# A top-k threshold search laid out by tokens, with seven candidates a round counted by TensorE, and one shared-expert group moved behind it

## The reference

```python
scores = jax.nn.sigmoid(h @ gate_w.T)                    # 2048 tokens x 16 experts
cap = math.ceil(T / E * TOP_K)                           # 256
topk_score, topk_ids = jax.lax.top_k(scores.T, cap)      # every expert takes 256 tokens
xin = h[topk_ids]
up = jnp.einsum('ecd,efd->ecf', xin, up_w) + up_b[:, None, :]
g = jnp.einsum('ecd,efd->ecf', xin, gw) + gb[:, None, :]
eo = jax.nn.silu(g) * up                                 # 512 hidden features
eo = jnp.einsum('ecf,edf->ecd', eo, down_w) + down_b[:, None, :]
flat = (eo * topk_score[..., None]).reshape(-1, Dm)
out = jnp.zeros_like(h).at[topk_ids.reshape(-1)].add(flat)
shared = jax.nn.silu(x @ sh_gate_w.T) * (x @ sh_up_w.T)  # 256 hidden features
out = out + shared @ sh_down_w.T
```

## Time and profile before

| what | value |
|---|---|
| timed runs, median of 3 | 206.12 us |
| profiled execution, span (first to last instruction) | 204.6 us |
| PE / PEld busy | 181.2 / 156.4 us |
| VectorE busy | 125.5 us |
| ScalarE busy | 90.3 us |
| GpSimd busy | 127.5 us |
| TensorE clock, mean over the span | 0.966 of full speed |

### The profile page before, as it was taken

One profiled execution on the slowest core, in us unless ns is written; L12 is line 12 of the kernel. 1 busy time (PEld: TensorE's weight loads), 2 busy tenths in 40 slices (PEclk: granted clock), 3 DMA queues, 4 the chain that ended last, 5 costly groups with the idle time before them and its releaser, 6 DMA issues.

```text
span 204.6 us, 3620 instructions
## 1 busy us (share of the span) xinstructions
PE 181.2 (89%) x1196; PEld 156.4 (76%) x1196; DVE 125.5 (61%) x430; ACT 90.3 (44%) x239; POOL 127.5 (62%) x195
## 2 busy tenths in 40 slices
PE   6979898999979999998999999999999999957800
PEld 6947688999936677857899999999999889945700
DVE  4888999999878787785667644454445344422300
ACT  0687512448697768110344344444444345422210
POOL 7494005556117475927777888878878777866660
PEclk9999999999999999999999999999999999995875
DMA  5599999800030271104313323333233333332221
GB/s 149 182 411 419 420 419 419 363 12 3 0 117 0 99 225 51 49 23 138 91 44 42 43 42 45 54 40 42 43 47 53 40 40 29 40 40 21 20 24 13
DMA packets 11649, 22.26 MB, mean 109 GB/s; under 512 B 1504, under 2 KB 8800, under 8 KB 11504
## 3 DMA queue, kind: packets, MB, share of 16 engines
q1 hardware_dynamic: 5968, 17.52, 22.7%
q0 software_dynamic: 5664, 4.53, 16.1%
HBM read 17.72 MB, written 4.33 MB: 108 GB/s over the span
## 4 chain that ended last, share of the span: by engine, by line
PE 41%; DMA 15%; POOL 14%; issue 11%; DVE 10%; ACT 4%; POOLq 1%; SPq 1%; DVEq 0%; ACTq 0%
DMA out_dram<-area,rows 13%; POOL out_dram L542 9%; PE bank L1155 7%; PE bank L1434 4%; PE bank L1110 4%; PE bank L1435 4%; POOL hT L531 4%; PE bank L1296 4%; PE bank L1415 3%; PE bank L1308 3%; DMA x_tok<-in_x_dram 2%; PE bank L1258 2%; DVE junk L950 1%; DVE area L807 1%; DVE hT L817 1%
## 5 line engine op out<-in xcount | busy, mean ns | idle before, releaser
L542 POOL DMA_INDIRECT out_dram<-area,rows x32 | 50.7, 1584 | 16.8 <-DMA out_dram<-area,rows 8.7
L1086 DVE SCALAR_TENSOR_TENSOR area<-bank,consts,sgate 128x256 f32<-128x256 f32 x64 | 30.9, 483 | 42.4 <-ACT sgate L734 42.1
L734 ACT ACTIVATE sgate<-bank,consts 128x256 f32<-128x256 f32 x64 | 30.3, 473 | 53.3 <-PE bank L1435 53.1
L1434 PE MATMUL bank<-area,wT 128*128 128x256 f32 x128 | 40.3, 397 | 4.8 <-issue 4.1
L1415 PEld LDWEIGHTS bank<-wT,area 128*128 128x128 f32 x256 | 38.1, 191 | 4.1 <-DVE area L1086 1.0
L531 POOL DMA_INDIRECT hT<-h_rows,rows x32 | 31.9, 995 | 12.7 <-issue 9.1
L1435 PE MATMUL bank<-area,wT 128*128 128x256 f32 x128 | 39.3, 390 | 0.0
L1415 PE MATMUL bank<-wT,area 128*128 128x128 f32 x256 | 38.6, 275 | 0.6 <-DVE area L1086 0.6
L1435 PEld LDWEIGHTS bank<-area,wT 128*128 128x128 f32 x128 | 25.2, 197 | 3.7
L1434 PEld LDWEIGHTS bank<-area,wT 128*128 128x128 f32 x128 | 20.5, 198 | 6.2 <-issue 5.7
L518 POOL TENSOR_TENSOR sh_hid<-sh_up,sgate 128x64 f32<-128x64 f32 x48 | 13.7, 322 | 14.6 <-ACT sh_up L686 12.1
(11 more groups left out here) (195 smaller groups left out, 259.1 us busy)
## 6 DMA issues: line engine op xcount, KB each, us to landing
wT<-in_weights_dram SPq DMA_DIRECT2D x16, 768.0 KB, 16.2
h_rows<-hrow SPq DMA_DIRECT2D x2, 576.0 KB, 3.7
x_tok<-in_x_dram SPq DMA_DIRECT2D x4, 256.0 KB, 3.9
x_tok<-in_down_b_dram SPq DMA_DIRECT2D x1, 1024.0 KB, 6.2
out_dram<-x SPq DMA_DIRECT2D x4, 256.0 KB, 2.1
hT<-h_rows,rows POOLq DMA_INDIRECT x32, 2.6
out_dram<-area,rows POOLq DMA_INDIRECT x32
sh_wT<-in_shared_dram SPq DMA_DIRECT2D x1, 384.0 KB, 2.9
```

Of the source, the lines that this page charges most:

```text
L542: pool.indirect_dma_start(out=out_rows, in_=eo[:, e % 2, c, :], in_offset=None, out_offset=bass.IndirectOffsetOnAxis(ap=rows[:, c, e:e + 1 ...
L734: act.activation(sgate_e[:, q % SGB, :], up_bank(q)[:, CAP:2 * CAP], ACT.Silu, bias=biasT[:, 1, j, e:e + 1]).then_inc(s_sil, 1)
L1086: dve.scalar_tensor_tensor(hidden[:, e % 2, j, :], up_bank(q)[:, 0:CAP], biasT[:, 0, j, e:e + 1], sgate_e[:, q % SGB, :], ALU.add, ALU.mul ...
L1434: pe.matmul(up_bank(q)[:, 0:CAP], wT[:, e, 0, j, :], xselT[:, e % 2, :], start=True, stop=True)
```

## The change

The scores stay as the router makes them: a partition holds 16 tokens with 16 experts each, 256 values, so nothing is turned. VectorE copies the high halves into `key_hi`. A round tries seven candidates (three bits) or three (two bits): one comparison of every key with every candidate, spread over the middle dimension, fills `over` with ones and zeros in 16 bits, 1792 or 768 per partition, in three pieces or two. TensorE multiplies a matrix of ones with `over`, 16 matmuls that add up in one PSUM row block, so that every partition gets all totals. VectorE compares them with 256, adds up the steps and makes the next candidates. There are eleven rounds: 8, 8, 8, 8, 4 for the high half and 8, 8, 8, 8, 4, 4 for the low one; between them `key_lo` is made by subtraction, joining and clamping. ScalarE counts no more. The masks come out by tokens and need no turning; column counts for the ranks go through TensorE and a copy of one column.

In the shared expert, groups 0 and 1 are projected in rounds 0 to 7, with outputs in rounds 6 to 10. Group 2 moves behind the search, with its product on VectorE (L1039 of the new file) instead of GpSimd, ahead of group 3. The warm-up matmuls in the rounds, ahead of the first table and behind the last spread are gone.

```diff
-        ROUNDS = [b for b in range(BITS - LOW - 2, -1, -2)] + [b for b in range(LOW - 2, -1, -2)]
+        ROUNDS = ((8, 2048), (8, 256), (8, 32), (8, 4), (4, 1), (8, 8192), (8, 1024), (8, 128), (8, 16), (4, 4), (4, 1))
+        ROUNDS_HIGH = 5
+        PIECES = {8: (0, 6, 12, 16), 4: (0, 10, 16)}
...
-            for n in range(LAST):
+            for n in range(LAST - 1):
                 for t in range(SHT):
                     pool.wait_ge(s_shsil, SHT * n + t + 1)
                     pool.wait_ge(s_shupe, SHT * n + t + 1)
...
                 if n:
                     shared_add(n - 1)
+            shared_add(LAST - 2)
...
-            act.wait_ge(s_scT, 1)
-            act.activation(score2[:, :].rearrange("p (t r) -> p r t", r=2), bank[5][:, 0:256].rearrange("p (r t) -> p r t", r=2),
-                           ACT.Sigmoid).then_inc(s_score, 1)
+            act.wait_ge(s_scaled, 1)
+            act.activation(score2[:, :], logits[:, :], ACT.Sigmoid).then_inc(s_score, 1)
...
+            def count(r, keys, cands):
+
+                n = ROUNDS[r][0] - 1
+                edges = PIECES[ROUNDS[r][0]]
+                for k0, k1 in zip(edges, edges[1:]):
+                    dve.tensor_tensor(over[:, k0 * n * E:k1 * n * E].rearrange("p (k c e) -> p k c e", c=n, e=E),
+                                      keys.rearrange("p (k e) -> p k e", e=E)[:, k0:k1, :].unsqueeze(2).to_broadcast(
+                                          [P, k1 - k0, n, E]),
+                                      cands[:, 0:n, :].unsqueeze(1).to_broadcast([P, k1 - k0, n, E]),
+                                      ALU.is_ge).then_inc(s_cnt, 1)
+
+            def settle(r, out):
+
+                radix, step = ROUNDS[r]
+                dve.wait_ge(s_tot, r + 1)
+                link(dve.tensor_scalar(steps[:, r % 2, 1:radix, :],
+                                       bank[5][:, 0:(radix - 1) * E].rearrange("p (c e) -> p c e", e=E), float(CAP),
+                                       float(step), ALU.is_ge, ALU.mult))
+                link(dve.tensor_reduce(out, steps[:, r % 2, 0:radix, :].rearrange("p c e -> p e c"), AX.X, ALU.add))
+
+            def next_cands(r):
+
+                radix, step = ROUNDS[r + 1]
+                link(dve.scalar_tensor_tensor(cand[:, 0:radix - 1, :], multiple[:, 0:radix - 1, :], float(step),
+                                              steps[:, (r + 1) % 2, 0, :].unsqueeze(1).to_broadcast([P, radix - 1, E]),
+                                              ALU.mult, ALU.add))
...
+                    link(dve.tensor_tensor(by_k(above), by_k(key_hi), found_hi[:, :].unsqueeze(1).to_broadcast([P, NT, E]),
+                                           ALU.subtract))
+                    link(dve.scalar_tensor_tensor(both[:, :], above[:, :], 65536.0, halves[:, 0, :], ALU.mult, ALU.add))
+                    link(dve.tensor_scalar(key_lo[:, :], both[:, :], 0.0, 65535.0, ALU.max, ALU.min))
...
+            shared_product(LAST - 1)
             times_token(1, 0, NT)
             for half in range(2):
                 hot_hi(1, half * NT // 2, (half + 1) * NT // 2)
...
+            shared_product(LAST)
             add_shared(LAST - 1, bank[4])
...
+            def count(r):
+
+                n = (ROUNDS[r][0] - 1) * E
+                edges = PIECES[ROUNDS[r][0]]
+                for k in range(NT):
+                    if k in edges:
+                        pe.wait_ge(s_cnt, pieces_until(r) + edges.index(k) + 1)
+                    last = pe.matmul(bank[5][:, 0:n], ones_b[:, :], over[:, k * n:(k + 1) * n], start=(k == 0),
+                                     stop=(k == NT - 1))
+                last.then_inc(s_tot, 1)
...
+            shared_down(1, 2)
+            shared_down(1, 3)
+            shared_up(2, 0, 0)
+            shared_up(2, 0, 1)
+            shared_up(2, 1, 0)
...
             table(0)
+            shared_up(2, 1, 1)
+            spread(0)
+            shared_up(LAST, 0, 0)
+            shared_up(LAST, 1, 0)
+            for t in range(4):
+                shared_down(LAST - 1, t)
             shared_up(LAST, 0, 1)
-            spread(0)
-            shared_up(LAST, 1, 0)
             shared_up(LAST, 1, 1)
             table(1)
-            pe.wait_ge(s_shsil, SHT * (LAST + 1))
             for t in range(4):
                 shared_down(LAST, t)
             spread(1)
-            stay_warm(WARM_E, bank[7])
```

More of the change, by code:

```diff
@@ L20 @@
 U16 = mybir.dt.uint16
+I16 = mybir.dt.int16
 P = 128
@@ new lines, in _ @@
+            keep_hT(0)
+            gate(0, 0)
+            keep_up(0, 0)
+            keep_hT(1)
+            gate(0, 1)
+            keep_up(0, 1)
+            features((4 * LAST, 4 * LAST + 1))
+            gate(1, 0)
+            keep_up(1, 0)
+            features((4 * LAST + 2, 4 * LAST + 3)).then_inc(s_hna, 1)
+            gate(1, 1)
+            keep_up(1, 1)
+            keep_hT(2)
+            keep_down(0)
+            keep_hT(3)
+            act.wait_ge(s_cntq, 1)
+            act.copy(cnt[:, 0:1], bank[6][:, 0:1]).then_inc(s_cntg, 1)
@@ L727, in _ @@
+            act.wait_ge(s_rank, 1)
+            act.copy(slot_a[:, :], ranks[0]).then_inc(s_slota, 1)
+            keep_down(1)
+            for n in (LAST - 1, LAST):
+                for t in range(SHT):
+                    gate(n, t)
             for q in range(E * FT):
@@ L933, in _ @@
                               ALU.mult).then_inc(s_scaled, 1)
             norm_shift(norm_no("x1", LAST))
-            low, high = halves[:, 0, :], halves[:, 1, :]
-            found_base, reached, cand, base, ktab, found = (search[:, a:b] for a, b in ((0, 1), (1, 2), (2, 5), (5, 8),
-                                                                                        (8, 11), (14, 15)))
-            for k in range(3):
-                dve.memset(ktab[:, k:k + 1], float(k + 1))
-                last = dve.memset(cand[:, k:k + 1], float((k + 1) << ROUNDS[0]) - 0.5)
@@ L1343, in _ @@
-            rank_base(0, 0, earlier)
-            pe.wait_ge(s_shupe, SHT * LAST)
-            rank_base(1, 0, same8_bf)
-            rank_base(1, 1, earlier)
-            for k in range(2):
-                pe.wait_ge((s_gtT, s_eqT)[k], 1)
-                pe.matmul(rank[k], lift[:, :], mask_T[:, k, :], start=False, stop=False, skip_group_check=True)
-                pe.matmul(rank[k][:, 0:P], ahead_of[:, :], mask_T[:, k, P:2 * P], start=False, stop=False,
-                          skip_group_check=True)
-                last = pe.matmul(rank[k][:, P:2 * P], until[:, :], mask_T[:, k, 0:P], start=False, stop=True,
-                                 skip_group_check=True)
-                last.then_inc(s_rank, 1)
@@ L1356, in _ @@
-            for t in range(4):
-                shared_down(LAST - 1, t)
-            shared_up(LAST, 0, 0)
-            stay_warm(WARM_I, bank[7])
+                    last = pe.matmul(bank[(6, 3)[k]][:, k:k + 1], picked[:, k, r * P:(r + 1) * P], ones_b[:, 0:1],
+                                     start=(r == 0), stop=(r == 1), skip_group_check=True)
+                last.then_inc(s_cntq, 1)
+                pe.matmul(ranks[k], lift[:, :], picked[:, k, :], start=True, stop=False, skip_group_check=True)
@@ new lines, in _ @@
+                pe.matmul(ranks[k][:, 0:P], ahead_of[:, :], picked[:, k, P:2 * P], start=False, stop=False,
+                          skip_group_check=True)
+                pe.matmul(ranks[k][:, P:2 * P], until[:, :], picked[:, k, 0:P], start=False, stop=False,
+                          skip_group_check=True)
+            pe.wait_ge(s_cntg, 1)
+            rank_base(0, 0, earlier, True).then_inc(s_rank, 1)
+            rank_base(1, 0, same_e, False)
+            pe.wait_ge(s_cnte, 1)
+            rank_base(1, 1, earlier, True).then_inc(s_rank, 1)
```

276 lines of the change are left out of this document (110 added, 166 removed).

## The result

The changed kernel took 211.21 us (median of 4 runs, 211.04 to 213.10), the kernel before on the same chip 206.25 (205.91 to 206.71). The ratio is 1.0257, interval 1.0216 to 1.0297. Measured again later it was 212.54 against 206.68: 1.0279, interval 1.0244 to 1.0314. The forecast was 212.9, in a range of 209.4 to 216.5: slower, as predicted, by 4.96 us instead of 6.75.

A forecast was written before the change was run, and what follows sets the result against it. Bound: GpSimd's gathers and scatters and TensorE's expert loop, meeting at expert 1, with GpSimd slower afterwards. Start 0, rounds +2.1, conflict +1.8 and loop +2.85 sum to +6.75 on 206.12: 212.9 us, range 209.4 to 216.5.

The forecast's parts named there:

- What sets the end: GpSimd's gather-scatter chain and TensorE's expert loop meet at expert 1; the later one's delay carries to the end undiminished.
- Rival 3: At the first scatters: they wait for the gathers alone, so the late loop is hidden; 209.2 us, chance 8%.
- Start: 0: Ahead of the first comparison: removed turn through TensorE and added 16-bit copy cancel; 0, between plus and minus 0.2 us.
- Rounds: +2.1: Search: eleven new rounds take 28.7 us against 26.57 for the old 15; +2.1, range +0.5 to +3.7.
- Conflict: +1.8: Search: GpSimd's products and addition delay VectorE's two-input instructions, 0.4 a round over 4.5 rounds; +1.8 us, ends 0.4 and 5.0.
- rival 2: Search: GpSimd blocks strictly, a whole piece ahead of each instruction; +5.0 in place of 1.8, 216.1 us, chance 8%.
- Masks: -0.4, off the path: Behind the search: first mask to slot numbers takes 2.0 us instead of 2.43; -0.4, not counted in the sum.
- Loop: +2.85: From search's end to the expert loop's start: 17.7 us instead of 14.84; +2.85, ends +2.1 and +3.6.
- Rival 1, the clock: Loop's lead-in: TensorE's clock falls to half speed for up to 6.8 us, costing 3.4; 216.3 us, chance 12%.
- Rival 4, a round costs its hand-over: Search: a round takes 1.65 to 1.8 us whatever its width, so the search gains 6.6; 202.9 us, chance 5%.

The follow-up runs named there:

- e1: Changed kernel with group 2 of the shared expert back between the search rounds, its product on GpSimd again; 208.54 us, ratio to before 1.0119.
- e3: Changed kernel with GpSimd's products of groups 0 and 1 and its additions replaced by fills that read nothing; 210.18 us, ratio to before 1.0192.
- e6: Changed kernel with 36 further GpSimd multiplications of 64 columns on a buffer of their own beside the search; 213.50 us, ratio to before 1.0341.
- e10: Changed kernel with GpSimd's two additions taken over by TensorE (product with the identity) and ScalarE (write); 211.14 us, ratio to before 1.0263.
- e5: Changed kernel with GpSimd's products of groups 0 and 1 in pieces of 256 columns instead of 64; 213.86 us, ratio to before 1.0346.
- e2: Kernel before, old search kept, with group 2 moved behind it and warm-up matmuls in its place in the last five rounds; 211.63 us, ratio 1.0247.
- e7: Old search with group 2 moved behind it, as e2, but two warm-up matmuls a round instead of six; 210.38 us, ratio to before 1.0195.
- e9: e1 with GpSimd's two additions taken over by TensorE (product with the identity) and ScalarE (write); 209.03 us, ratio to before 1.0119.

## Why the prediction was right, and where not

- *What sets the end.* Right. Scatters 0 and 1 wait for ScalarE, from expert 2 on GpSimd is held by its own work, and the shift of 4.92 comes out as 4.93 at scatter 2 and as 5.0 of span. Rival 3 (gathers alone) falls by the wait of 3.30; e1 shows the point at which it would start to hold, a loop start 3.5 us earlier, where the two chains are level.
- *Start: 0.* Measured -0.47; 0.32 of it is there already at the logits, and logits start anywhere from 53.09 to 53.77 in the variants with the same work ahead of them, so most is not the change's.
- *Rounds: +2.1.* Without conflict they cost +1.23 (e3: 27.80). The round of eight was right in its sum (2.73 against 2.72), partly by luck: it is 1.70 and not 1.80 to the totals, and 1.02 and not 0.93 behind them. The rounds of four were mis-sized: 1.61 and 1.86, where 1.87 and 2.12 were forecast, and 2.73 with the step between the halves instead of 2.97. That is 0.24 to 0.26 in each of three, nearly all of the 0.9. The failing part is the way from the first comparison to the totals: 0.33 + 0.14 + 0.60 + 0.32 = 1.39 was forecast, 81.60 - 80.52 = 1.08 measured. I had sixteen matmuls at 0.04 in a row behind the first piece and a whole hand-over after them; in fact VectorE is done with both pieces in 0.63 and waits only 0.45 for the totals.
- *Conflict: +1.8.* 1.39 in the search. The price of a hit, 0.1, was right (though the two late instructions that it was read from stood beside additions, 74.88 to 76.57 and 83.62 to 85.32, and not beside a product), as was 0.4 for a round that GpSimd fills (0.33 in e6). What failed is the count: a product is 2.8 us long but meets the chain twice, some 0.23 a product and not 0.4 a round. The dear part is one that I had as a by-thing: the two additions with pieces of 128 columns cost 0.4 in the search (e10) and 0.61 among the tables (e3). By the rule of the Trainium skill ("SBUF — State Buffer", section Who interferes with whom) the later of the two engines' instructions is blocked until the other's is done: e5 agrees that the wait follows the length of the piece (0.53 for 256 columns). Taken as one full wait for every instruction it gave 5.0, and rival 2 with it falls.
- *Masks: -0.4, off the path.* The size was right (0.54), the place was not: e2 with the old masks shows it in the lead-in, and the loop's own sum had it in already, with its ranks at 1.5.
- *Loop: +2.85.* Measured 2.77. It is some 3.3 from the move of group 2 (e1: 3.19 back, e2: 3.35 there) less the masks' 0.5; the second addition among the tables (0.61) is part of it, as its upper end had it. The near hit of the middle is partly luck: its 17.7 had no addition in it, and without one the lead-in is 17.00 (e3), so its other steps were 0.7 too long in sum.
- *Rival 1, the clock.* In the changed kernel it stayed at 1.00 through search and lead-in; e5 and e7 fell to 1.2 GHz there (0.53 and 0.50 in a stretch of 2 us) and paid 1.0 and 0.65. The danger was real and priced too high at 3.4.
- *Rival 4, a round costs its hand-over.* Falls: rounds of four and eight differ by their width, 1.86 and 2.72.

The terms that were too large, 0.5 of start, 0.9 of rounds and 0.4 of conflict, make up the 1.8 us between 6.75 and 4.92.

## What to carry to other kernels

Price a search by what a bit costs, not by how many rounds go: three bits for 2.72 us and two for 1.77 are the same bargain, and then what had to move out of the rounds decides. Work that is moved behind a serial stage is paid nearly in full if the next stage starts on the same engine (3.2 of the 3.7 us of four projections), even where the stage that it leaves could have held it for nothing, as e1 did. Where VectorE's instructions have two inputs in SBUF, keep GpSimd's pieces beside them short and few. And read a gain ahead of the loop at scatter 2, ahead of the waits for landings that vary, not from the time alone.

## What was not expected of the hardware

- The hit by a GpSimd piece grows with the piece: 0.08 to 0.12 us at 64 columns, about 0.2 at 128 (the last round's two comparisons 1.05 instead of 0.63 beside an addition), 0.53 at 256. Two inputs are not needed for it: an instruction with one 16-bit input took 0.47 beside the second addition, 0.22 without (e3). GpSimd pays as well: a product of eight pieces takes 2.74 to 2.90 beside the new comparisons, 2.28 beside the old.
- A scatter's landing is late by some 2 us once in a while (the next one waited 2.65 in e9 and 2.54 in e2, where 0.6 to 0.8 is usual as long as a gather stands between them), and I found nothing in the traces that goes with it. It hid gains of half a microsecond ahead of the loop. What causes it stays open.
